# Three of the sixteen last tiles masked and added by Pool instead of DVE

## The reference, cut to what matters

```python
x = x + gelu(norm(x) @ (w1 @ w2.T * sparse_mask) + b2)
x = x + ffn(norm(x))
x = x + attention(norm(x))
x = x + ffn(norm(x))

def ffn(x):                        # x is [tokens, 512]
    dots = softmax(x @ centroids.T / 0.1)
    hits = dots > 0.01
    query_sel = any(hits, axis=1)           # one flag per token
    row_sel = any(hits, axis=0)[assignments] # one flag per output column
    dense = x @ weight.T + bias
    return where(query_sel[:, None] & row_sel[None, :], dense, 0)
```

## Time and profile before

| | us |
|---|---|
| three runs | 277.4, 278.08, 1536.68 |
| their median | 278.08 |
| the profiled execution, its own time | 277.66 |
| its span | 275.9 |
| busy: PE, DVE, ACT, POOL | 269.5, 195.2, 176.7, 158.9 |

### The profile page before, as it was taken

The page is one execution under the profiler, slowest core; times in us unless marked ns, Lnnn a source line. Parts: engine busy times, 40 slices in busy tenths (PEclk is TensorE's granted clock), DMA queues, the critical chain, the costliest instruction groups (busy, mean ns, idle before and its releaser), DMA issues.

```text
span 275.9 us, 4431 instructions
## 1 busy us (share of the span) xinstructions
PE 269.5 (98%) x1398; PEld 224.7 (81%) x1398; DVE 195.2 (71%) x410; ACT 176.7 (64%) x358; POOL 158.9 (58%) x192
## 2 busy tenths in 40 slices
PE   8899999999999999999999999999999999999994
PEld 8687888888888888788988888888888888887673
DVE  3887988605935867785389796788349475967996
ACT  4855886365477786448899988778555567575400
POOL 4793888175395491189896893980640438113730
PEclk9999999999999999999999999999999999999999
DMA  6999054800000000000000000000000000000087
GB/s 229 365 364 334 23 200 185 301 4 0 2 0 0 2 0 2 0 2 0 2 0 0 1 4 0 2 0 0 5 0 0 0 2 0 1 2 0 17 305 288
DMA packets 10246, 18.23 MB, mean 66 GB/s; under 512 B 1200, under 2 KB 1968, under 8 KB 10224
## 3 DMA queue, kind: packets, MB, share of 16 engines
q1 hardware_dynamic: 10224, 17.96, 18.3%
HBM read 13.76 MB, written 4.19 MB: 65 GB/s over the span
## 4 chain that ended last, share of the span: by engine, by line
PE 92%; DVE 4%; DMA 1%; issue 1%; SPq 0%; ACT 0%; DVEq 0%; ACTq 0%
PE m_bank L965 72%; PE t_bank L1058 11%; PE m_bank L1138 5%; DMA x_tok<-in_L_attn_a_x 1%; PE t_bank L1064 1%; PE m_bank L1018 1%; DVE y_tok L924 1%; DVE st L767 1%; DVE qsel L896 0%; ACT ce L670 0%; DVE x_tok L948 0%; SPq L383 0%; DVE y_tok L935 0%; PE m_bank L1085 0%; DVE cl L880 0%
## 5 line engine op out<-in xcount | busy, mean ns | idle before, releaser
L965 PE MATMUL m_bank<-ffn_hi,even_hi 128*128 128x512 f32 x96 | 39.0, 406 | 0.2 <-DVE y_tok L924 0.2
L965 PE MATMUL m_bank<-ffn_lo,even_hi 128*128 128x512 f32 x96 | 37.6, 392 | 0.0
L965 PE MATMUL m_bank<-ffn_hi,even_lo 128*128 128x512 f32 x96 | 37.4, 390 | 0.0
L545 POOL TENSOR_TENSOR y_tok<-y_tok,x_tok 128x512 f32<-128x512 f32 x16 | 20.3, 1291 | 25.5 <-ACT y_tok L718 25.5
L569 ACT ACTIVATE ones_and_squares<-x_tok,mv 128x512 bf16<-128x512 f32 x44 | 31.5, 717 | 4.1 <-DVE x_tok L871 3.7
L525 POOL TENSOR_TENSOR y_tok<-y_tok,bias_f 128x512 f32<-128x512 f32 x16 | 20.5, 1290 | 16.2 <-ACT y_tok L663 16.2
L453 POOL TENSOR_SCALAR ve<-mv 128x1 f32<-128x1 f32 (+1 forms) x20 | 5.3, 264 | 36.6 <-ACT ones_and_squares L569 35.6
L457 POOL TENSOR_TENSOR rstd<-ve,half 128x1 f32<-128x1 f32 (+1 forms) x31 | 23.8, 769 | 2.6
L774 DVE TENSOR_TENSOR even_lo<-t_bank,even_hi 128x512 fp32r<-128x512 f32 x24 | 16.2, 683 | 12.8 <-ACT even_hi L612 12.6
L774 DVE TENSOR_TENSOR odd_lo<-t_bank,odd_hi 128x512 fp32r<-128x512 f32 x28 | 18.8, 686 | 6.4 <-ACT odd_hi L612 6.1
L965 PE MATMUL m_bank<-odd_hi,wqkv_hi 128*128 128x512 f32 (+1 forms) x60 | 21.5, 358 | 0.0
(11 more groups left out here) (186 smaller groups left out, 776.0 us busy)
## 6 DMA issues: line engine op xcount, KB each, us to landing
out<-x_tok SPq DMA_DIRECT2D x15, 256.0 KB, 2.3
x_tok<-in_L_attn_a_x SPq DMA_DIRECT2D x3, 1024.0 KB, 9.0
xn_odd<-in_L_attn_a_xt SPq DMA_DIRECT2D x2, 1024.0 KB, 7.1
x_tok<-in_L_attn_a_x SPq DMA_DIRECT2D x4, 256.0 KB, 4.2
y_tok<-in_L_attn_a_w SPq DMA_DIRECT2D x4, 256.0 KB, 5.0
w_raw<-in_L_attn_a_w SPq DMA_DIRECT2D x4, 256.0 KB, 5.1
xt_other<-in_L_ffn_weight SPq DMA_DIRECT2D x4, 256.0 KB, 6.4
y_tok<-in_L_attn_a_sparse_mask SPq DMA_DIRECT2D x4, 256.0 KB, 6.8
```

What stands on the lines that cost most here:

```text
L545: pool.tensor_tensor(y_tok[:, n, :], y_tok[:, n, :], x_tok[:, n, :], ALU.add).then_inc(done[kind], 1)
L965: ins = pe.matmul(bank, a, w, start=(first and n == 0), stop=(last and n == count - 1))
```

## The change

The set `BY_POOL` names three tiles: (1,3), (2,3) and (3,2). For these

- Pool's `xb` is dropped, so y_tok holds only the bias times the query flag when `blend4` adds the product; `blend4` waits for `qb` instead of `xb`;
- PE makes the mask a second time into a bank of the other rotation (`masks.4`, right behind `mask.4`), and ACT copies it into `rows` in SBUF (`rows4`, last in its list);
- Pool multiplies y_tok by `rows` (`pm`) and adds it to x_tok (`pa`), as the last six steps of its list, in the order (2,3), (1,3), (3,2);
- DVE's `out` is dropped, and SP's store waits for `pa`; the stores are in a new order, and so are the lists of DVE (three steps less) and Pool.

```diff
--- before.py
+++ after.py
@@ -24,6 +24,8 @@
 T_BANKS = 4
 M_BANKS = 4
 WARM = 13
+
+BY_POOL = {(1, 3), (2, 3), (3, 2)}
 
 SQUARED = {2, 3, 4}
 
@@ -55,7 +57,7 @@
 T.p.3.1 dn4.1.2.c3 dn4.1.3.c32 dn4.1.2.c102 dn4.1.0.c1 T.x4.2.2 T.x4.2.3 T.x4.2.0 wo.2.1 pv.3.h01 dn4.1.1.c012
 wo.3.2 wo.3.0 dn4.1.1.c3 T.x4.2.1 wo.3.3 T.x4.3.0 T.x4.3.2 wo.3.1 cl4.2.h01 T.x4.3.1 T.x4.3.3 tc.4.2 dn4.2.3.c2
 cl4.3.h0 dn4.2.1.c1 cl4.3.h1 dn4.2.1.c2 tc.4.3 dn4.2.1.c3 dn4.2.3.c1 dn4.2.1.c0 dn4.3.0.c2 dn4.2.3.c0 dn4.3.0.c0
-dn4.2.3.c3 dn4.3.0.c31 dn4.3.2.c2 bestT.4 dn4.3.1.c0 dn4.2.2.c1 mask.4 dn4.3.1.c1 dn4.3.2.c03 dn4.2.2.c3
+dn4.2.3.c3 dn4.3.0.c31 dn4.3.2.c2 bestT.4 dn4.3.1.c0 dn4.2.2.c1 mask.4 masks.4 dn4.3.1.c1 dn4.3.2.c03 dn4.2.2.c3
 dn4.3.1.c3 dn4.3.2.c1 dn4.3.1.c2 dn4.2.0.c312 dn4.2.2.c20 dn4.2.0.c0 dn4h.3.3.0 dn4h.3.3.1
 """
 
@@ -81,7 +83,7 @@
 hi.x4.1.2 ohi.2 sq.4.1.1 exp.3.3 vev.3 hi.p.3.2 sq.4.1.0 exp.3.1 hi.p.3.3 lgev.4.1 cexp.4.1 hi.p.3.0 hi.v.3.0
 qb.1.1 qb.1.3 sq.4.2.3 qb.1.0 hi.p.3.1 qb.1.2 sq.4.2.2 hi.x4.2.2 hi.x4.2.3 sq.4.2.1 hi.x4.2.0 ohi.3 sq.4.2.0
 sq.4.3.2 hi.x4.2.1 sq.4.3.0 hi.x4.3.2 sq.4.3.3 hi.x4.3.0 lgev.4.2 hi.x4.3.1 hi.x4.3.3 sq.4.3.1 cexp.4.2 lgev.4.3
-qb.2.0 qb.2.1 cexp.4.3 qb.2.3 qb.3.0 qb.3.1 qb.3.3 qb.3.2 qb.2.2
+qb.2.0 qb.2.1 cexp.4.3 qb.2.3 qb.3.0 qb.3.1 qb.3.3 qb.3.2 qb.2.2 rows4
 """
 
 DVE_ORDER = """
@@ -106,9 +108,9 @@
 lo.x4.1.1 olo.2 lo.x4.1.2 max.3.1 x3.2.3 lo.p.3.3 lo.p.3.2 logit.4.1 lmax.4.1 x3.2.0 x3.2.2 prob.4.1 lo.v.3.0
 rden.3 blend4.1.3 lo.p.3.0 lo.p.3.1 x3.2.1 blend4.1.0 blend4.1.2 lo.x4.2.3 olo.3 lo.x4.2.2 lo.x4.2.0 x3.3.2
 x3.3.0 blend4.1.1 lo.x4.2.1 x3.3.3 lo.x4.3.2 x3.3.1 lo.x4.3.0 lo.x4.3.1 logit.4.2 lmax.4.2 lo.x4.3.3 prob.4.2
-logit.4.3 lmax.4.3 prob.4.3 blend4.2.3 best1.4 blend4.2.1 csel.4 blend4.3.0 out.0.1 out.2.3 out.0.0 out.1.1
-out.1.0 out.0.2 blend4.3.2 out.1.3 out.3.2 out.3.0 out.0.3 out.2.1 blend4.3.1 out.1.2 blend4.2.0 blend4.2.2
-out.2.0 out.3.1 blend4h.3.3.0 out.2.2 blend4h.3.3.1 outh.3.3.0 outh.3.3.1
+logit.4.3 lmax.4.3 prob.4.3 blend4.2.3 best1.4 blend4.2.1 csel.4 blend4.3.0 out.0.1 out.0.0 out.1.1 out.1.0
+out.0.2 blend4.3.2 out.3.0 out.0.3 out.2.1 blend4.3.1 out.1.2 blend4.2.0 blend4.2.2 out.2.0 out.3.1
+blend4h.3.3.0 out.2.2 blend4h.3.3.1 outh.3.3.0 outh.3.3.1
 """
 
 POOL_ORDER = """
@@ -121,16 +123,16 @@
 masked.2.1 bias2.2.3 masked.2.2 masked.2.3 rstd.3.2.0 rstd.3.2.3 masked.3.0 bias2.3.2 rstd.3.2.1 rstd.3.2.2
 bo.0.2 bo.0.1 masked.3.2 bo.0.0 bias2.3.3 bo.0.3 bias2.3.1 masked.3.3 rstd.3.3.3 masked.3.1 rstd.3.3.0 bo.1.0
 rstd.3.3.2 bo.1.1 bo.1.2 rstd.3.3.1 bo.1.3 bo.2.1 bo.3.0 rstd.4.0 xb.0.1 bo.2.0 bo.2.3 xb.0.3 xb.0.2 xb.0.0
-rstd.4.1 bo.2.2 bo.3.2 bo.3.3 xb.1.3 xb.1.1 bo.3.1 xb.1.2 xb.1.0 rstd.4.2 rstd.4.3 xb.2.1 xb.2.3 xb.3.0 xb.2.0
-xb.3.2 xb.3.3 xb.3.1 xb.2.2
+rstd.4.1 bo.2.2 bo.3.2 bo.3.3 xb.1.1 bo.3.1 xb.1.2 xb.1.0 rstd.4.2 rstd.4.3 xb.2.1 xb.3.0 xb.2.0 xb.3.3 xb.3.1
+xb.2.2 pm.2.3 pa.2.3 pm.1.3 pa.1.3 pm.3.2 pa.3.2
 """
 
 SP_ORDER = """
 load.x0.0 load.w1.0 load.w2.0 load.x0.1 load.x0.2 load.w1.1 load.x0.3 load.w2.1 load.w2.2 load.w1.2 load.w1.3
 load.w2.3 load.ffn.1 load.ffn.0 load.cen load.ffn.2 load.sparse.0 load.ffn.3 load.sparse.1 load.sparse.2
 load.sparse.3 load.small load.x.1 load.b2 load.xt.1 load.x.3 load.late load.x.2 load.bias load.xt.2 load.xt.3
-store.2.3 store.1.0 store.0.0 store.0.1 store.1.3 store.3.2 store.1.1 store.0.3 store.2.1 store.3.0 store.0.2
-store.1.2 store.2.0 store.3.1 store.2.2 storeh.3.3.0 storeh.3.3.1
+store.1.0 store.0.0 store.0.1 store.1.1 store.0.3 store.2.1 store.3.0 store.0.2 store.2.3 store.1.2 store.1.3
+store.2.0 store.3.2 store.3.1 store.2.2 storeh.3.3.0 storeh.3.3.1
 """
 
 def steps_of(text):
@@ -149,7 +151,7 @@
 SP_STEPS = steps_of(SP_ORDER)
 
 PARTS = {"y1": KC, "dn2": KC, "dn4": KC, "cl2": 2, "cl4": 2, "q": 2, "k": 2, "v": 2, "pv": 2}
-T_KINDS = ("T", "tc", "bestT", "colmean", "ffnmean")
+T_KINDS = ("T", "tc", "bestT", "colmean", "ffnmean", "masks")
 M_KINDS = ("last", "y1", "dn2", "dn4", "dn4h", "cl2", "cl4", "q", "k", "v", "sc", "pv", "wo", "mask")
 
 
@@ -367,7 +369,10 @@
             for kind, key in SP_STEPS:
                 if kind == "store":
                     b, t = key
-                    sp.wait_ge(*done_at("out", (b, t)))
+                    if key in BY_POOL:
+                        sp.wait_ge(*done_at("pa", key))
+                    else:
+                        sp.wait_ge(*done_at("out", key))
                     sp.dma_start(out_d[b, t * P:(t + 1) * P, :], x_tok[:, b * TPB + t, :]).then_inc(stored, 16)
                     continue
                 if kind == "storeh":
@@ -543,6 +548,17 @@
                     pool.wait_ge(*done_at("qb", (b, t)))
                     pool.wait_ge(*done_at("x3", (b, t)))
                     pool.tensor_tensor(y_tok[:, n, :], y_tok[:, n, :], x_tok[:, n, :], ALU.add).then_inc(done[kind], 1)
+                elif kind == "pm":
+                    b, t = key
+                    n = b * TPB + t
+                    pool.wait_ge(*done_at("rows4", ()))
+                    pool.wait_ge(*done_at("blend4", key))
+                    pool.tensor_tensor(y_tok[:, n, :], y_tok[:, n, :], rows[:, :], ALU.mult).then_inc(done[kind], 1)
+                elif kind == "pa":
+                    b, t = key
+                    n = b * TPB + t
+                    pool.wait_ge(*done_at("pm", key))
+                    pool.tensor_tensor(x_tok[:, n, :], x_tok[:, n, :], y_tok[:, n, :], ALU.add).then_inc(done[kind], 1)
 
         @block.scalar
         def _(act):
@@ -674,6 +690,10 @@
                     act.wait_ge(*done_at("x2", *[(0, t) for t in every]))
                     act.wait_ge(*done_at("scaled", *[(NB - 1, t) for t in every]))
                     act.activation(rows[:, :], bank_of("mask", 2)[:, :], ACT.Copy).then_inc(done[kind], 1)
+                elif kind == "rows4":
+                    act.wait_ge(*done_at("masks", (4,)))
+                    act.wait_ge(*done_at("masked"))
+                    act.activation(rows[:, :], bank_of("masks", 4)[:, :], ACT.Copy).then_inc(done[kind], 1)
                 elif kind == "qkhi":
                     w, b = key
                     j = "qk".index(w)
@@ -919,7 +939,10 @@
                     b, t = key
                     n = b * TPB + t
                     dve.wait_ge(*done_at("dn4", key))
-                    dve.wait_ge(*done_at("xb", key))
+                    if key in BY_POOL:
+                        dve.wait_ge(*done_at("qb", key))
+                    else:
+                        dve.wait_ge(*done_at("xb", key))
                     dve.wait_ge(*done_at("prob", (4, b)))
                     dve.scalar_tensor_tensor(out=y_tok[:, n, :], in0=bank_of("dn4", *key)[:, :], scalar=rq[:, 1, n:n + 1],
                                              in1=y_tok[:, n, :], op0=ALU.mult, op1=ALU.add).then_inc(done[kind], 1)
@@ -981,6 +1004,8 @@
                     return done_at("fcent")
                 if kind == "mask":
                     return done_at("rows", ())
+                if kind == "masks":
+                    return done_at("rows4", ())
                 return done_at(freed_by[kind], key)
 
             rotation = {True: [g for g in BANK if g[0] in T_KINDS], False: [g for g in BANK if g[0] not in T_KINDS]}
@@ -1077,6 +1102,10 @@
                     pe.wait_ge(*done_at("slo", ()))
                     pe.matmul(bank, mean_of[:, :], a_sum_hi, start=True, stop=False)
                     pe.matmul(bank, mean_of[:, :], a_sum_lo, start=False, stop=True).then_inc(done[kind], 1)
+                elif kind == "masks":
+                    bank = bank_for("masks", *key)
+                    pe.wait_ge(*done_at("csel", key))
+                    pe.matmul(bank[:, :], csel[:, :], onehot[:, :], start=True, stop=True).then_inc(done[kind], 1)
                 elif kind == "mask":
 
                     bank = bank_for("mask", *key)
```

## The result

The changed kernel took 278.74 us (median of 12 runs, 277.73 to 279.51), the kernel before 278.12 beside it: a ratio of 1.0026 with a 95% interval of 1.0013 to 1.0038, so about 0.7 us slower. (Two runs of the kernel before, of 339.46 and 1536.68 us, stay out of the ratio; the median of the other ten is 278.03.) Measured again later beside other kernels it was 1.0007 (0.9986 to 1.0027), which no longer excludes that nothing changed. It is no change by the 2% mark, and a small loss by the first measurement. The forecast was 277.7 with a range up to 278.7; the median lies just outside. The execution that the profile shows took 278.26, against 277.66 before: 0.60 more, like for like.

The account below looks back on a forecast made before the run. PE, busy 98%, bounds the kernel except the last 20 us, whose end the last half store's issue sets. PE's gain of 0.41 against 0.40 for the extra stored tile sums to 0.0: 277.66 + 0.0 = 277.7 us, range 276.9 to 278.7.

Parts of the forecast that it names:

- Rival 2: qsel's length not Pool's doing, or another wait holds PE at 256.5: slower, 278.3 us; chance 0.26.
- DVE's three copies are worth 0 on the path: Last stage: dropping three predicated copies, 1.95 us, only adds DVE idle before waits for PE; worth 0.
- Rival 3: DVE bounds the last stage after all, so all 1.95 us comes off: 275.7 us; chance 0.04.
- qsel sits out Pool's `xb.2.3`: Block 3's short DVE comparison at 253.65 waits for a Pool operation, taking 1.30 us instead of 0.17.
- g = 0.41: PE's head start in us from the next product after the mask; bounds -0.34 to 0.69.
- Pool's tail ready at 264.3, 266.8, 269.4: End of Pool's list: times when tiles (2,3), (1,3) and (3,2) would be ready for their stores.
- Rival 4: Pool late at 1.6 us an operation beside DVE, holding up the last stores: 279.6 us; chance 0.03.
- The extra tile in the last burst costs 0.40 against the lead: Final stores: a further full tile costs 0.69 us, of which 0.3 fits in the gap of 273.10 to 273.40.
- the lead: PE's gain of 0.41 us after the mask, kept until the last blends and the final stores' issue.
- Rival 1: The final burst of stores fits in and PE's whole gain of 0.41 us arrives: 277.25 us; chance 0.20.
- PE: one matmul `masks.4` with the same weights and 512 columns: 0.23.: Added PE matmul behind the mask's: costs 0.23 us, 0.34 if first after a stall, 0 if PE would wait.
- From 271.77 - g the queues get four full tiles without a gap: Final stores: four full tiles take 2.75 us and two halves 0.92, so data end at 275.03.

Follow-up runs that it names:

- experiment 4: Changed kernel with an extra, unused Pool multiply where `xb.2.3` had stood; 278.14 us, ratio 0.9993 to the kernel before.
- experiment 6: Changed kernel without TensorE's repeated waits, all matmuls kept; 277.47 us, ratio 0.9979 to the kernel before.
- experiment 7: Changed kernel without TensorE's repeated waits and with the store of (3,2) ahead of (2,0); 277.21 us, ratio 0.9969 to the kernel before.
- experiment 8: Kernel before, with TensorE's repeated waits left out; 277.26 us, ratio 0.9973 to the unaltered kernel before.
- experiment 9: Changed kernel with only tile (2,3) on Pool and without TensorE's repeated waits; 277.14 us, ratio 0.9971 to the kernel before.
- experiment 12: Changed kernel with only tile (2,3) on Pool and all TensorE waits kept; 277.58 us, ratio 0.9990 to the kernel before.
- experiment 5: Changed kernel measured again without any edit; 278.47 us, ratio 1.0007 to the kernel before.
- experiment 3: Changed kernel with the store of (3,2) ahead of the store of (2,0); 277.56 us, ratio 0.9986 to the kernel before.
- experiment 2: Kernel before with 17 instead of 13 warm-up matmuls, lengthening TensorE's program; 278.61 us, ratio 1.0005 to the unaltered kernel before.

## Why the prediction was wrong

Point by point. The forecast of 277.7 was 1.04 below the measured median, for two reasons. The change itself, forecast at 0.0, was 0.62 by the medians (278.12 and 278.74) and 0.60 by the profiled executions (277.66 and 278.26). The other 0.4 lies in where the sum started: it took the profiled execution, 277.66, which lay 0.42 below the median known then (278.08), as the prediction said itself. From that median the forecast would have been 278.1, still 0.6 too low, and a range shifted along with it would have ended at 279.1. (Rival 2 and the spread, 278.3 and 0.3, make 278.6, not 278.7; nothing hangs on that.)

- *DVE's three copies are worth 0 on the path.* Right: the idle time before the two waits grew by 0.85 and by over a microsecond, and no blend started sooner for it. Rival 3 (DVE the bound, 275.7) is out.
- *qsel sits out Pool's `xb.2.3`, g = 0.41.* Right, 0.44, and experiment 4 shows the cause. The Trainium skill's rule (SBUF — State Buffer, "Who interferes with whom"), that the holder keeps the shared port for its whole instruction, is borne out: qsel ends 0.03 after Pool in the kernel before and in experiment 4, whatever Pool's operation lasts (1.28 and 1.04). So is the half that cleared the change, that copies under a mask in PSUM pass: five in 3.28 beside Pool.
- *Pool's tail ready at 264.3, 266.8, 269.4.* Right (the last at 269.60). Rival 4 is out.
- *The extra tile in the last burst costs 0.40 against the lead.* The term was right in kind, its size 0.3 (0.28 between experiments 6 and 7). In the terms of the prediction the end would be 0.14 earlier than before, had there been nothing else: the forecast of 0.0 was 0.14 too high here. Rival 1, that the burst fits in and costs nothing, is out.
- *"PE: one matmul `masks.4` with the same weights and 512 columns: 0.23."* This is the step that failed. As time on TensorE it is right to the hundredth. But the instruction was costed only as time on its engine and not as length of its program. The page of before lists the instruction queues (q8 with 11 packets), and the argument passed over them. With the added instructions there is a 12th packet, and where it falls into the last burst it adds 0.6 to 0.9 us to the stores, more than the lead gave. In the prediction's sum it is the stores' term that breaks: "From 271.77 - g the queues get four full tiles without a gap", data end at 275.03. They had a gap from 272.5 to 273.0 (share 0.35) and a lone engine behind it, and the data ended at 275.70. This is shown for the profiled execution; that the 0.7 of the median has the same cause is likely, not shown.

Rival 2 named a time near the measured one (278.3) for another reason: that the lead wouldn't come. It came. A time that fits a rival is no witness for it; the two distances were.

The Trainium skill, Runtime: NRT & Kernel Launch, section "Instruction fetch mechanics", says that each engine refills its instruction memory in blocks of 16 KiB, 256 instructions, through a DMA queue of its own, and that this is hidden since instructions are issued more slowly than they are fetched. The traces agree with the size (0.20 MB in 12 packets, some 17 KB each) and show no idle time of TensorE at the fetch of 270.94. They add, as read from the lone engine and the long issue, what the section doesn't weigh: the block goes over one of the DMA engines that the stores use, so it is hidden from the engine that runs the program and not from SP.

What stays open: why the times fall by some 0.2 to 0.3% where TensorE's repeated waits are left out of the kernel before (experiment 8), in what share of executions the 12th fetch meets the last burst, and with that whether it makes the median's loss.

## What to carry to other kernels

An instruction has a second price besides its time: it lengthens its engine's program, and the program is fetched, as these traces are read, over the same DMA engines that move the data; look at the packets of the instruction queues on the page, and keep such a fetch out of the last burst of stores (here by leaving out waits that are already met). Work moved to an idle engine is worth nothing where the busy one waits anyway; what paid here was that one Pool operation no longer stood beside a short DVE operation on the critical path, and one tile moved does that without adding a tile to the last burst (experiments 9 and 12; the 0.4 us show in the tail and are too small for the times). When an effect is smaller than the scatter of the times, compare distances between fixed steps inside the trace: here they repeated to 0.05 us while the times scattered by 2.

## What the runs showed of the hardware

- One packet of instructions, which took 0.9 to 1.1 us in the tails, can hold up the stores behind it: in the changed kernel SP's next issue took 1.18 us instead of about 0.4, in experiment 5 one took 0.91, in experiments 3 and 4 one took 1.45, and in experiment 3 only one engine's worth of work went on for a microsecond (share 0.06, 14 GB/s) while half a tile was still to be written. In experiment 2 no issue was long, and the store part grew by 0.7 all the same.
- The moment of a fetch moves between executions of the same length of program by some microseconds: 270.9, 271.0, 273.4 and 276.5 for the 12th in kernels with the changed TensorE list, and 176.1, 180.1 and 182.4 for the 8th in three executions of the kernel before.
- A DVE comparison of 128x4 that starts within 0.01 us of a Pool operation of 128x512 takes as long as that operation, 1.30 and 1.06 for 1.28 and 1.04, against 0.17 alone.
